# Decoder layer on one core: the gates' results in the buffer of the last stage, and the first group's normalized rows read back in the setup's fourth round

## The reference

```python
x = x + attn(layernorm(x), Wq, Wk, Wv, Wo, Wa, Wb, conv weights)   # gated delta rule, 16 heads
x = x + xattn(layernorm(x), ctx_512, ctx_512)                      # 32 query heads, 8 key heads
x = x + ffn(layernorm(x), w1, b1, w2, b2)                          # ternary weights, gelu
# in attn, for each head:
q, k = l2norm(silu(conv(x @ Wq))), l2norm(silu(conv(x @ Wk)));  v = silu(conv(x @ Wv))
alpha, beta = sigmoid(x @ Wa), sigmoid(x @ Wb)
# scan over tokens: state = state * alpha; err = v - state.k; state += beta * k err; out = state.q
```

## Time and profile before

| | us |
|---|---|
| median of 3 runs | 2485.99 (2484.18 to 2489.06) |
| profiled execution, its time | 2486.33 |
| profiled execution, span from first to last instruction | 2484.7 |
| PE busy | 2146.1 (86%) |
| DVE busy | 1858.5 (75%) |
| ACT busy | 1473.8 (59%) |
| POOL busy | 1090.4 (44%) |
| mean granted TensorE clock | 0.968 |

### The profile page before, as it was taken

How to read it: one execution, slowest core, us unless ns; L and a number is a source line. 1 busy time by engine, 2 the same in 40 slices (tenths; PEclk the granted TensorE clock), 3 DMA queues, 4 the chain that set the end, 5 groups by cost and what they waited for, 6 DMA issues and landing times.

```text
span 2484.7 us, 66235 instructions
## 1 busy us (share of the span) xinstructions
PE 2146.1 (86%) x23576; PEld 1370.0 (55%) x23576; DVE 1858.5 (75%) x2925; ACT 1473.8 (59%) x2755; POOL 1090.4 (44%) x1440
## 2 busy tenths in 40 slices
PE   2376769989998898999899899999988888999998
PEld 2133335555555565555555555555555567777776
DVE  7675667978887787888779788888856556776665
ACT  3475646666666666666566666666656535555554
POOL 1015574654737366373736638374571012222222
PEclk9898989999999999999999999999989999999999
DMA  7546543233333324333332433333242110111100
GB/s 289 160 106 135 124 93 83 85 84 93 85 83 92 84 76 89 87 85 83 91 85 76 91 89 82 90 94 85 69 90 61 37 55 12 32 40 41 33 20 18
DMA packets 507447, 205.37 MB, mean 83 GB/s; under 512 B 437584, under 2 KB 462928, under 8 KB 505168
## 3 DMA queue, kind: packets, MB, share of 16 engines
q1 hardware_dynamic: 507088, 200.76, 32.0%
HBM read 128.33 MB, written 72.35 MB: 81 GB/s over the span
## 4 chain that ended last, share of the span: by engine, by line
PE 51%; DVE 12%; issue 12%; SPq 10%; ACT 8%; DMA 5%; POOL 1%; ACTq 0%; DVEq 0%; POOLq 0%
PE PS L1278 15%; PE PS L1292 9%; DVE Y L1028 6%; PE PS L1516 3%; PE PS L1356 3%; PE PS L1445 3%; PE PS L1478 3%; PE PS L1372 2%; PE PS L1329 2%; SPq L377 2%; PE PS L1506 2%; ACT XN L796 2%; DMA SCR<-PGD 2%; PE PS L1464 2%; SPq L431 2%
## 5 line engine op out<-in xcount | busy, mean ns | idle before, releaser
L1028 DVE SCALAR_TENSOR_TENSOR Y<-PS,CW,Y 128x504 f32<-128x504 f32 (+2 forms) x1536 | 1115.4, 732 | 404.5 <-ACT Y L770 350.7
L770 ACT ACTIVATE Y<-PS,CW 128x512 f32<-128x512 f32 x512 | 398.5, 778 | 395.1 <-PE PS L1278 384.6
L1292 PE MATMUL PS<-WOS,XN 128*128 128x256 f16 x3072 | 389.7, 278 | 4.3 <-DVE XN L1043 3.3
L1292 PEld LDWEIGHTS PS<-WOS,XN 128*128 128x128 f16 x3072 | 307.0, 100 | 108.1 <-issue 12.1
L1278 PE MATMUL PS<-XV,WH 128*128 128x512 f16 x1024 | 322.2, 398 | 32.3 <-DMA XV<-XHD 20.1
L1278 PE MATMUL PS<-XK,WH 128*128 128x512 f16 x1024 | 312.5, 387 | 16.3 <-DMA XK<-XHD 16.2
L632 POOL TENSOR_TENSOR SQ<-KQ 128x512 f32<-128x512 f32 x128 | 138.1, 1079 | 427.5 <-PE PS L1320 335.7
L618 POOL TENSOR_TENSOR SCR<-SCR 128x31 f32<-128x31 f32 (+15 forms) x496 | 282.1, 569 | 38.9
L615 POOL TENSOR_TENSOR SCR<-SCR 128x31 f32<-128x31 f32 (+15 forms) x496 | 268.7, 542 | 33.0
L796 ACT ACTIVATE XN<-PS,KN 128x256 f32<-128x256 f32 x512 | 212.6, 466 | 71.7 <-PE PS L1292 71.7
L1043 DVE TENSOR_TENSOR XN<-Y,XN 128x512 f16<-128x512 f32 x256 | 202.8, 792 | 12.5 <-ACT Y L777 12.5
(11 more groups left out here) (141 smaller groups left out, 3124.9 us busy)
## 6 DMA issues: line engine op xcount, KB each, us to landing
PGD<-SCR SPq DMA_DIRECT2D x128, 256.0 KB, 2.2
SCR<-PGD SPq DMA_DIRECT2D x128, 256.0 KB, 3.0
EQD<-XN SPq DMA_DIRECT2D x32, 512.0 KB, 4.1
SCR<-EQD SPq DMA_DIRECT2D x128, 128.0 KB, 2.8
SCR<-QND SPq DMA_DIRECT2D x128, 128.0 KB, 3.2
SCR<-in_wall SPq DMA_DIRECT2D x8, 1024.0 KB, 5.9
SCR<-PGD SPq DMA_DIRECT2D x64, 128.0 KB, 3.3
ED<-SCR SPq DMA_DIRECT2D x16, 512.0 KB, 2.7
```

The source lines that it names most:

```text
L770: A_.activation(Y[:, b, :], PJ[b][:, :], ACT.Identity, scale=CW[:, h[1] % NH, cw0 + 3:cw0 + 4], bias=CW[:, h[1] % NH, cw0 + 4:cw0 + 5]).th ...
L1028: V_.scalar_tensor_tensor(yv[:, :, m:T], pv[:, :, 0:T - m], CW[:, h[1] % NH, cw0 + 3 - m:cw0 + 4 - m], yv[:, :, m:T], ALU.mult, ALU.add).t ...
L1292: ins = mm(VWB[:, E * i:E * i + E], VHL[:, vk, n, P * a:P * a + P], WOS[:, wk, 2 * (w[1] % NH) + n, :], start=(t == 0), stop=(t == 5))
```

## The change

`BEA` becomes a view of `VB` in place of the second half of `XK`, so `XK` is not written in the setup any more. The load of `XK` for group 0 moves from behind the wait for the stores into round four of the setup (g == 3), behind the load of the last block of `wall`; ahead of it stands a wait for the store of `XHD[0]`. The load of `XV` stays where it was.

```diff
-        XKF = XK[:, :, :].rearrange("p c t -> p (c t)").bitcast(F32)
-        BEA = XKF[:, 512:1024].rearrange("p (g h a) -> p g h a", g=G, a=NP)
+        BEA = VB[:, :, :, :].rearrange("p n g d -> p (n g d)")[:, 0:512].rearrange("p (g h a) -> p g h a", g=G, a=NP)
...
+                if g == 3:
+                    sp.wait_ge(S["st_xh0"], at(16))
+                    sp.dma_start(XK[:, :, :], XHD[0]).then_inc(S["ld_xk"], 16)
...
             stored_eq(NP)
-            sp.dma_start(XK[:, :, :], XHD[0]).then_inc(S["ld_xk"], 16)
             sp.dma_start(XV[:, :, :], XHD[0]).then_inc(S["ld_xv"], 16)
```

## The result

| | before | after |
|---|---|---|
| median, us | 2486.05 (20 runs, 2479.5 to 2497.46) | 2479.39 (20 runs, 2465.71 to 2488.79) |
| ratio | | 0.9967, 95% interval 0.9951 to 0.9983 |
| span of the profiled execution | 2484.7 | 2467.8 |

The changed kernel is faster by 8.2 us by the ratio (4.2 to 12.2), by 6.7 by the medians. The forecast was 10.9. So the first thing to read is where in the span the two part.

What follows compares the result with a forecast made beforehand. The prediction took a chain of single steps through PE's 10.7 us wait for the late `XK` load as the bound. Its terms, -11.4 + 0.5 = -10.9 us from the median of 2485.99, gave 2475.1, range 2469.5 to 2481.

Steps and rivals of the forecast that it cites:

- A: Theory tested by the experiments: the 11 to 12 us shift lasts to the end; executions of one program differ by some us.
- PE's wait goes: At PE's first projection: the 10.7 us idle wait for `XK` vanishes, so PE starts at 102.76 instead of 113.45.
- What is late next: At the first head: DVE, ending its sum over `w2` at 107.29, is the last to be ready; key's tap at 106.1.
- The size of the shift: At the query's convolution: start moves from 122.12 to 110.70, 11.4 us earlier: 9.7 for DVE's wait, 1.7 for its pause.
- The `EQD` loads: Before `decayed_grams`: issued at 110.0, the first lands at 114.4, 2.1 us before it is needed.
- Rival (b): At `decayed_grams`: the `EQD` loads become the gate, 2.3 us too late at twice 4.4, giving 2477.4; chance 0.03.
- The setup's cost: In setup round five: the 512 KB `XK` transfer delays the x load by 0.5 us, bounds 0 to 1.5.
- Rival (a): In setup rounds five and six: the transfer costs 1.5 us in each, 3.0 instead of 0.5, giving 2477.6; chance 0.05.
- The clock in PE's new work: At the first head on PE: each projection priced at full clock, 1.31 us, and a decay unit at 2.15.
- Rival (c): At PE's first projection: something else also holds PE to about 109.5, so only 3.7 us go, giving 2482.8; chance 0.04.
- Rival (d): In the main part: TensorE's mean clock falls by 0.01, costing 16 us and giving 2491, slower; chance 0.04.
- its small form: In the main part: shifted stalls change the mean clock slightly, some us either way; range allows some 0.003 of mean clock.

Runs made afterwards that it cites:

- The moved sum: The changed kernel with DVE's sum over `w1` moved behind the first key's convolution and the mask of unit 5; ratio 0.9946, 13.4 us faster than before.
- after again: The changed kernel with no edit, run and profiled a second time; ratio 0.995, 12.4 us faster than before, profile span 2477.7.

## Why the prediction was right, and where it wasn't

The forecast of 2475.1, 10.9 below before, lies in the interval of the measured gain (4.2 to 12.2), though 2.7 above its middle. The changed kernel measured again gained 12.4, that with the load behind `w1` 11.7. These intervals are 8 us wide, so the times alone hardly test the sum; the distances in the profiles do. By them the change takes out 10.7 us in the mean and costs 1.0 in the setup, 9.7 together, where the forecast had 11.4 and 0.5. Of the two theories, A holds so far as the runs go, with a shift of 10.1 to 11.6 in place of 11 to 12: the shift is in every profile, what was added at the same place arrived at the end, and the main part is no longer for the change. A loss of 1 or 2 us isn't excluded.

- **PE's wait goes.** Right: the key's projection follows unit 3's last matmul (102.26) at 102.47, with no idle time.
- **What is late next.** Right in the engine, and in the changed kernel's times: ACT's unit 4 at 107.08 (forecast 107.2), the tap at 108.05 (108.3), the query's `conv` at 110.40 (110.70). The moved sum shows that DVE was the one, and that the tap would be next 1.4 us earlier; the forecast had 1.2 (107.29 - 106.1).
- **The size of the shift.** Of the forecast's 11.4, 9.7 are DVE's wait, which is as long in all three profiles (9.73, 9.75, 9.55). The other 1.7 are a pause that only the first profile of before has in this length; the other two have 0.22 and 0.48. One profile was read as the kernel. The mean over the three is 10.7.
- **The `EQD` loads.** Right: issued at 109.80, landing 3.7 us later at 113.5, needed at 116.22. Rival (b) is out. With `XK` gone from the queue they were faster than 4.4.
- **The setup's cost.** Forecast 0.5 (0 to 1.5), found 1.0 in the mean of three profiles. The mechanism was right: the x load of round five takes 4.9 to 5.1 where the five profiles without the load have 4.0 to 4.3. That the next round gives part of it back is seen in one profile alone (4.44 in round six; the others have 5.44 and 7.15, without the load it is 5.3 to 6.0). Rival (a), the cost twice over (3.0), isn't the mean, but one of the three profiles, at 2.4, comes near it. The end of the last sum, which was to read off this cost, lies between 107.3 and 108.6 in the four kernels without an early load, and so can't tell it.
- **The clock in PE's new work.** The two projections and the unit that the forecast priced at the full clock did run at it (1.00 from 103 to 107.4). What it left out is the projection behind them, the next head's key. In after PE waited for DVE ahead of it, and the clock stood near half from there on:

```profile
107.40:109.50 2.10, 0.01 (x1) 0.04 (x2) 2.03 (x4) 2.08 (x4) 0.31 (x1) 1.00 0.74 152
109.50:113.20 3.70, 3.70 (x8) 1.53 (x9) 3.09 (x4) 1.76 (x3) 0.00 (x0) 0.54 0.71 227
```

The wait was 2.1 us, and this third projection ran at a granted clock of 0.54. So the Gram product began at 114.72, 1.4 behind the end of silu (112.70 + 0.63), and not at once, as the forecast says. DVE's next `conv` reached to 116.2 anyway, so `decayed_grams` didn't wait, and the step had no effect.
- **GpSimd.** Left out: the first square was counted among the things that shift. It doesn't. The square began 7.25 us after the all-reduce, which had been hidden in the 16.29 us that GpSimd waited in before:

```profile
124.12 1.04 POOL L632 TENSOR_TENSOR SQ<-KQ 128x512 f32<-128x512 f32 x1 [16.29 <-ACT KQ L784]
```

Here it cost nothing, but with little to spare: the square ends at 115.99 and PE's sum of it begins at 117.14. With the all-reduce where it is, 1.2 us more gained in front would have made this the limit, ahead of the tap at 1.4; the moved sum shows what it costs then.
- **Rival (c)** is out by PE's start. **Rival (d)**, the clock of the main part, didn't go against the change, but its small form is larger than the forecast allowed for: 0.003 of mean clock were put at some 5 us, and two profiles of one program differ by 8.8 in the main part. My own criterion, that the distance from the query's `conv` to the end must not change by over 5 us, was therefore too narrow for one pair of profiles, and the first profile of after misses it: it is 2362.6 in before, 2357.4 in after (2467.8 - 110.40) and 2365.6 in after again (2477.7 - 112.07), on either side.

## What to carry to other kernels

A load that stands late only because something else lies in its buffer is worth moving to where its source is ready, and its gain is not the wait shown at one engine (10.7) but the distance to what is late next on each engine behind it, read in more than one profile (here 10.1, 10.2 and 11.6, up to DVE's sums). Price its new place by the free share of the queue up to the next load that is waited for, and expect to pay part of the transfer even where the free time would hold it: here 512 KB of 1.5 us cost about 1 us, alone or as one of four. And before a whole span is compared, compare stage by stage, with a second profile of the same program beside it: here the stage that no edit touched moved by up to 14 us, more than the edit was worth.

## What the runs showed of the hardware

- After a `partition_all_reduce` GpSimd began its next `tensor_tensor` 7.0 to 7.7 us later in five profiles, with the input there (7.25, 7.34, 6.97, 7.66, 7.26). This time moves with the all-reduce and stays hidden where GpSimd waits anyway (16.29 us in before).
- The same 1.7 ms of instructions on one core took 1707.6 to 1721.8 us, with 82 to 109 us at half clock.
- One to four 512 KB loads ahead of an x load cost about 1 us each: 1.0 in the mean for one (33.9 to 34.9), 3.6 for four (37.5).
- The clock stood near half in after from 109.5 to 113.2 (0.54), behind an idle time of PE of 2.1 us, with PE busy for 4.38 of the 4.40 us before that.
- PE began at half clock behind its wait of 10.5 to 10.7 us in three profiles, and was back at full after 5.9, 2.9 and 3.5 us of work.
